# Key stacks of 48 stored rows, with their rows of ones written on chip, in a two-layer attention and expert kernel

## What is computed

```python
x = L0_attn_x
xn = _layernorm(x, axis=-1)
s = attention with 16 heads of 8 channels on xn
g = _silu(mixture of experts on xn)
x = x + s * g
```

## Time and profile before

| | us |
|---|---|
| median of 3 runs | 1200.33 (1199.22 to 1203.84) |
| the profiled execution | 1205.69 |
| its span in the trace | 1203.9 |
| PE busy | 1068.8 |
| DVE busy | 814.8 |
| ACT busy | 646.0 |
| POOL busy | 201.9 |

### The profile page before, as it was taken

The page is one execution under the profiler, slowest core; times in us unless marked ns, Lnnn a source line. Parts: engine busy times, 40 slices in busy tenths (PEclk is TensorE's granted clock), DMA queues, the critical chain, the costliest instruction groups (busy, mean ns, idle before and its releaser), DMA issues.

```text
span 1203.9 us, 19384 instructions
## 1 busy us (share of the span) xinstructions
PE 1068.8 (89%) x7308; PEld 496.2 (41%) x7308; DVE 814.8 (68%) x1621; ACT 646.0 (54%) x1258; POOL 201.9 (17%) x323
## 2 busy tenths in 40 slices
PE   5799999999999999999864799889989999988767
PEld 4455555552222222222233343334444478444444
DVE  6656666667887888883377587888872255565654
ACT  4522222217898888989622256667775533432534
POOL 2244554510010101011000001123320000000000
PEclk9799999999999999999976688999997999998888
DMA  4674121000110110000034013211322020000431
GB/s 117 206 227 140 49 79 66 1 10 19 30 42 29 43 32 27 18 13 21 10 122 142 28 39 80 76 48 50 129 97 80 11 79 1 1 1 0 142 141 35
DMA packets 57398, 74.63 MB, mean 62 GB/s; under 512 B 15720, under 2 KB 35032, under 8 KB 55512
## 3 DMA queue, kind: packets, MB, share of 16 engines
q1 hardware_dynamic: 48516, 62.13, 16.2%
q10 hardware_dynamic: 8788, 11.26, 3.2%
HBM read 58.18 MB, written 14.54 MB: 60 GB/s over the span
## 4 chain that ended last, share of the span: by engine, by line
PE 70%; DVE 18%; ACT 7%; issue 3%; DMA 1%; ACTq 0%; SPq 0%; POOL 0%; DVEq 0%
PE PS L1806 68%; DVE mx L1575 9%; ACT arena L1074 5%; PE PS L1819 1%; DVE arena L1374 1%; DVE arena L1780 1%; PE PS L2278 0%; DVE arena L1377 0%; DVE arena L1338 0%; DVE arena L1326 0%; DVE small L1766 0%; DMA arena<-mrow 0%; DMA arena<-in_L_attn_x 0%; ACT arena L1027 0%; DVE fw L1671 0%
## 5 line engine op out<-in xcount | busy, mean ns | idle before, releaser
L1806 PE MATMUL PS<-arena 128*32 128x512 f32 (+12 forms) x3656 | 565.8, 474 | 60.9 <-DVE mx L1575 23.4
L1575 DVE TENSOR_REDUCE mx<-PS 128x1 f32<-128x512 f32 (+3 forms) x896 | 512.3, 623 | 82.8 <-PE PS L1806 78.6
L1074 ACT ACTIVATE arena<-PS 128x512 f32<-128x512 f32 (+3 forms) x896 | 435.4, 559 | 149.7 <-PE PS L1806 145.7
L1806 PEld LDWEIGHTS PS<-arena 128*32 128x32 f32 (+3 forms) x3656 | 147.1, 104 | 416.9 <-ACT arena L1074 183.8
L1806 PE MATMUL PS<-x_hi,w_hi_lo 128*128 128x512 f32 x320 | 145.5, 496 | 7.0 <-POOL x_lo L991 2.6
L1117 ACT ACTIVATE fw<-PS 128x512 f32<-128x512 f32 x80 | 47.8, 597 | 168.1 <-PE PS L1806 168.1
L1671 DVE TENSOR_TENSOR fw<-PS,fw 128x512 f32<-128x512 f32 x80 | 55.3, 692 | 79.1 <-PE PS L1806 75.1
L1806 PE MATMUL PS<-fw 128*128 128x512 f32 (+3 forms) x184 | 99.2, 625 | 0.0
L985 POOL TENSOR_TENSOR fw<-fw,arena 128x512 f32<-128x512 f32 x64 | 81.8, 1280 | 75.7 <-DVE fw L1671 75.7
L917 POOL TENSOR_TENSOR arena<-arena,fw 128x512 f32<-128x512 f32 x31 | 39.8, 1284 | 296.6 <-DMA fw<-sum_dram 296.6
L1806 PEld LDWEIGHTS PS<-x_hi,w_hi_lo 128*128 128x128 f32 x320 | 61.2, 191 | 38.4 <-issue 21.5
(11 more groups left out here) (315 smaller groups left out, 1113.9 us busy)
## 6 DMA issues: line engine op xcount, KB each, us to landing
arena<-comb_dram SPq DMA_DIRECT2D x14, 1024.0 KB, 4.9
arena<-comb_dram SPq DMA_DIRECT2D x18, 512.0 KB, 7.3
fw<-sum_dram SPq DMA_DIRECT2D x31, 256.0 KB
q_dram<-arena SPq DMA_DIRECT2D x24, 256.0 KB, 4.0
k_dram<-arena SPq DMA_DIRECT2D x24, 256.0 KB, 4.2
arena<-k_dram ACTq DMA_DIRECT2D x20, 204.0 KB
arena<-q_dram ACTq DMA_DIRECT2D x20, 192.0 KB
arena<-drev_dram SPq DMA_DIRECT2D x16, 192.0 KB, 6.8
```

The lines of the kernel that those rows point to most:

```text
L1074: s.activation(Pr[:, m % 8, 0:w], st_bank(l, m, 0, w), ACT.Exp).then_inc(A["e_done"], 1)
L1575: v.reduce_max(mx[:, H % 2, kh, n:n + 1], bank(ring_bank[l][U], 0, w), axis=AX.X, negate=True).then_inc(A["ring_free"], 1)
L1806: return nc.tensor.matmul(out_, lhsT, rhs, start=start, stop=stop)
```

## The change

The key stacks are stored with 48 rows, so that the DMAs of store_qk write with another stride and those of load_group read 48 rows (192 KB) instead of 51. The two DMAs that stored the rows of ones are gone. In their place POOL sets whole regions of the arena to one before any key stack is loaded into them: 16 KiB of each of the 128 partitions (8192 bf16 elements) from 48 KiB on, at the start, after the memsets of Vst; and the same amount from 32 KiB on in layer 1's attention, after the maxima of H = 0 and 1 and before the loop over the halves. A load overwrites 48 rows at partition 0 and 48 at partition 64; the three rows after each keep their ones. SP and ACT wait for the first memset where they waited for the stores of ones, and ACT waits for the second before it loads group 4 of layer 1. The old ones region (96 x 1024 bf16) and POOL's wait behind it are gone. The matmuls are the same.

```diff
-        k_dram = [dram(f"k_dram{l}", (GROUPS * HG, TROWS, SEQ), BF16) for l in range(2)]
+        k_dram = [dram(f"k_dram{l}", (GROUPS * HG, ROWS, SEQ), BF16) for l in range(2)]
...
-        ones_rows = bf(62, 2)[0:32 * PARTS, :]
+        ones_rows = [bf(48, 16), bf(32, 16)]
...
-                dr, rows, at_ = ((q_dram[l], ROWS, q_at[l]), (k_dram[l], TROWS, k_at[l]))[piece % 2]
-                src = bass.AP(tensor=dr.tensor, offset=(G * HG + hh) * rows * SEQ,
-                              ap=[[SEQ, rows], [2 * rows * SEQ, PAIRS], [1, SEQ]])
-                dst = bf(at_[G], 4)[64 * hh:64 * hh + rows, :].rearrange("p (r t) -> p r t", r=PAIRS)
+                dr, at_ = ((q_dram[l], q_at[l]), (k_dram[l], k_at[l]))[piece % 2]
+                src = bass.AP(tensor=dr.tensor, offset=(G * HG + hh) * ROWS * SEQ,
+                              ap=[[SEQ, ROWS], [2 * ROWS * SEQ, PAIRS], [1, SEQ]])
+                dst = bf(at_[G], 4)[64 * hh:64 * hh + ROWS, :].rearrange("p (r t) -> p r t", r=PAIRS)
...
-            sp.wait_ge(zero_done, 3)
-            for l in range(2):
-                dst = bass.AP(tensor=k_dram[l].tensor, offset=ROWS * SEQ, ap=[[TROWS * SEQ, GROUPS * HG], [SEQ, PARTS], [1, SEQ]])
-                sp.dma_start(dst, ones_rows).then_inc(ones_stored, 16)
             store_qk(sp, 0, 0)
...
-            sp.wait_ge(ones_stored, 16 * 2)
+            sp.wait_ge(ones_set, 1)
...
                 for H in range(LAG[l]):
                     max_parts(H)
+                pool.wait_ge(z_ready, 12)
+                g.memset(ones_rows[1], 1.0).then_inc(ones_set, 1)
                 for H in range(HALVES):
...
             pool.wait_ge(const_done, 1)
-            g.memset(ones_rows, 1.0).then_inc(zero_done, 1)
-            pool.wait_ge(zero_done, 3)
             own.link(g.memset(Vst[:, :, :, :, :], 0.0))
             own.link(g.memset(Vst[:, :, :, :, HD:HD + 1], 1.0))
...
+            g.memset(ones_rows[0], 1.0).then_inc(ones_set, 1)
             weights_lo(0)
...
-            act.wait_ge(ones_stored, 16 * 2)
+            act.wait_ge(ones_set, 1)
...
                 act.wait_ge(last_norm, 1)
+                act.wait_ge(ones_set, 2)
                 next_group(1, 4, (0, 1))
```

More of the change, by code:

```diff
@@ L472, in block_net @@
             "lg_ps", "gx_ready", "ge_ready", "comb_ready", "cb_ps", "cb_ev"))
-        comb_stored, ones_stored = sem("comb_stored"), sem("ones_stored")
+        comb_stored, ones_set = sem("comb_stored"), sem("ones_set")
         rows_ps, rows_ev = sem("rows_ps"), sem("rows_ev")
@@ L614, in store_qk @@
                 for n in range(parts):
-                    dst = bass.AP(tensor=k_dram[l].tensor, offset=(b * HEADS * TROWS + (row + n) * HD) * SEQ,
-                                  ap=[[TROWS * SEQ, HEADS], [SEQ, HD], [1, SEQ]])
+                    dst = bass.AP(tensor=k_dram[l].tensor, offset=(b * HEADS * ROWS + (row + n) * HD) * SEQ,
+                                  ap=[[ROWS * SEQ, HEADS], [SEQ, HD], [1, SEQ]])
                     src = kspb[b][:, n, :] if l else ksp[:, n, b * SEQ:(b + 1) * SEQ]
```

## The result

| | before | after |
|---|---|---|
| median of 6 runs each, us | 1201.16 (1199.06 to 1203.84) | 1208.49 (1207.02 to 1210.19) |
| the profiled execution, us | 1205.69 | 1207.02 |
| its span, us | 1203.9 | 1205.2 |

The ratio is 1.006, with a 95% interval of 1.0041 to 1.008: the change costs 7.2 us. Lines of the kernel after are 2 to 4 lower (L1332 is the L1334 of before, L1804 its L1806, L1071 its L1074, L679 and L597 are unchanged).

A forecast was written before the change was run, and what follows sets the result against it. PE (70% of the chain of waits) and DVE (18%) were taken to bound the kernel; +5.2 - 3.0 + 2.2 = +4.4 us on 1200.33 gave 1204.7 us, with 8 in 10 for 1197.0 to 1211.0.

The forecast's parts named there:

- Spared stores: At the start, dropping the two stores of ones from SP's queue gains nothing, since the serial start covers them.
- First memset: At the start, POOL's 6.97 us memset holds DVE's tensor_scalar L1334 until 15.93 instead of 10.72, delaying the serial start: +5.2 us.
- rival of a clock that falls at the later start: After longer PE idling at the start, a low clock doubles 3.4 us of projection matmuls: +7.8 at most, chance 0.10.
- Two-input instructions held as well: Rival: beside the first memset DVE's two-input instructions also wait, +5.8 in place of +5.2, 1205.3 us, chance 0.05.
- Short hold: Rival: DVE gets in between parts of the long first memset, so the sum is -1.8, 1198.5 us; chance 0.15.
- Maxima rows: At layer 1's attention start, 48-row key loads finish before the maxima rows load, so PE goes on earlier: -3.0 us.
- rival of late rows: At layer 1's attention start, group loads still collide with the maxima rows; the 3.0 is not gained: +7.4, chance 0.15.
- Second memset: In layer 1's attention, POOL's 6.97 us memset exceeds 4.70 us idle, delaying PE's matmul of the H = 2 maxima: +2.2 us.
- Key loads elsewhere are covered: Key loads away from layer 1's start change nothing, as PE is the chain while layer 0's groups 1 to 3 load.
- other waits between 54 and 600 us: Sign of a wrong forecast: new waits in PE's list in this stretch, where the same time as before was expected.
- a fifth of 0.55: Share of the forecast (0.50) and two-input (0.05) cases counted as slower by over 0.5%, put at 0.12.

The follow-up runs named there:

- e1: Kernel after, first memset written as float32 words holding two bf16 ones, half by DVE early and half by POOL: ratio 1.0023 to before.
- e4: Kernel before plus one POOL memset of 8192 bf16 elements in an unused region, behind the memsets of Vst: ratio 1.0049, +5.9 us.
- e8: Kernel before with 48-row key stacks only in layer 1, its memset between the maxima of H = 0 and 1: ratio 0.9980, -2.4 us.
- e2: Kernel after with POOL's second memset moved between the maxima of H = 0 and 1: ratio 1.0044 to before.
- e12: Kernel before plus only the second memset (8192 bf16 elements, behind the maxima of H = 0 and 1): ratio 1.0017, +2.0 us.
- e7: Kernel after with 48-row key stacks only in layer 0, first memset split between DVE and POOL, no second memset: ratio 1.0025 to before, +3.0 us.
- e10: Kernel after with layer 0's loads of groups 4 to 7 issued by SP instead of ACT, both long memsets kept: ratio 1.0032 to before.
- e3: Kernel after with first memset split between DVE and POOL and second memset between the maxima of H = 0 and 1: ratio 1.0004 to before.
- e5: e3 with layer 0's loads of groups 4 to 7 issued by SP instead of ACT: ratio 0.9989 to before, -1.3 us.
- e11: e5 with the second memset written as 4096 float32 words holding two bf16 ones: ratio 0.9979 to before, -2.5 us.

## Why the prediction was right in part, and what it missed

The direction and the range held, and so did the terms of the first memset and of the maxima rows; the second memset was right in its mechanism and uncertain in its size. The size of the whole did not hold: 4.4 us were forecast and 7.2 came, which is just over 0.5%, where I had thought a change within 0.5% likelier. Step by step:

- **Spared stores: nothing.** No run takes this by itself, and none tells against it; SP's new waits appear nowhere in the chain.
- **First memset, +5.2 us: right.** Its length 6.92 us (forecast 6.97), its place 8.94 (8.93), L1332's end 15.89 (15.93). Of the 5.17 us, 3.8 are left when PE takes over; the ratios give 4.4 (after against e1). The rival of a clock that falls at the later start did not come: transposes and projections ran at 1.00, as before. It had priced the eight projections at 3.4 us; they took 4.24 before and 3.45 after.
- **Two-input instructions held as well: false.** They took 0.17 and 0.19 us in the memset. The Trainium skill's rule on this ("GPSIMD Engine Reference", section Key points) counts both kinds; beside a memset the measurement decides against it for two-input instructions. The Trainium skill also says ("VectorE: DVE Perf Modes", section Mode 2×_2P — use both read ports for one tensor) that a float32 tensor_scalar from SBUF uses both read ports, which tensor_tensor can't. The trace agrees with the half that concerns the tensor_scalar: 6.35 us for one that takes 0.17.
- **Short hold: false**, from the same line, and e4 shows it with nothing else changed.
- **Maxima rows, -3.0: right**, -2.73 in the chain's piece (4.50 to 1.77), -2.4 by e8's ratio. The piece is 4.01 to 4.53 us in the five traces with 51 rows in layer 1 and 1.77 to 1.80 in the nine with 48. The rival of late rows had asked for under 150 GB/s; the loads moved at 154 to 217 in the full windows and were nearly over when the last of the maxima loads was issued at 681.90.
- **Second memset, +2.2: the mechanism right, the size at most that.** PE waits for POOL behind the memset, and the two matmuls are 8.20 to 8.21 us apart in all four kernels with the memset at this place. Against the kernel before that is +1.94. But 6.26 us is the shortest such distance of all ten kernels without it; the others have 6.81 to 7.66, and e2, which only moves the memset, has 7.33. So the memset's own price was 0.5 to 1.9 us, 0.9 by e2's trace. The ratios (+2.0 by e12, +1.9 by e2) are within their intervals of all of this. The prediction let the memset fill 4.70 us of idle time that it had from a single trace.
- **"Key loads elsewhere are covered: PE is the chain while groups 1 to 3 of layer 0 come in": the step that failed.** It looked at the transfers of three groups and at nothing that issues them. Groups 4 to 7 of layer 0 are issued by ACT between exponentials that PE waits for, and for these I had put nothing. In the trace after, six of these eight key issues take 0.44 or 0.45 us and two 0.98 and 1.26, where seven took 0.33 and one 0.54; the two long ones stand in the chain. Price: +3.0 by e7, +3.4 by e10, and +1.3 to +3.2 us between the marks in the five traces that have these issues. The prediction had named the sign, other waits between 54 and 600 us, where it expected the same time as before. In the kernel before nothing shows that an issue can take 1.0 us, but the row of ACT's 0.33 us for group 2 was there, and a bound from it (eight key issues of layer 0, each doubled: 8 x 0.33 = 2.6 us) would have put the sum at 7.0; the doubling is chosen with hindsight.

By the ratios the sum now reads 4.4 + 2.0 + 3.2 - 2.4 = 7.2 us: first memset, second memset, layer 0's issues (mean of e7 and e10), maxima rows. It meets the measured 7.2. The terms come from different sittings and each has an uncertainty of 2 to 3 us, and the traces have less for the second memset, so the close meeting is luck in part; what carries the account is that every term has its line in a trace and that each taken away alone moved the time the way it should. One slip in the chances changes nothing: a fifth of 0.55 is 0.11, not 0.12.

Open: why some back-to-back issues take 0.44 us and others 0.98 to 1.57. In e7 three of the first five take 0.88 or more, in e3 two, with the same loads. Part of the cost in layer 0 is the clock that falls behind a long stop (0.50 at 406 to 408 us after and at 400 to 402 in e7, 0.56 at 400 to 402 in e1, 1.00 all along in e2 and e3). Layer 0's attention costs 2.9 to 3.2 us more in the three traces where it falls and 1.3 and 1.8 in the two where it doesn't; what decides whether it falls is open.

## What to carry to other kernels

A transfer that is hidden still has an issue, and that one lies on the engine that issues it: when a DMA's shape changes, read the duration of its issue and ask what is queued behind it, or spread the issues, or give them to an engine that nobody waits for. A long memset on POOL is not free in POOL's idle time: choose a time at which DVE runs no tensor_scalar from SBUF, and write float32 words that hold two bf16 values, which halves it. Price a fill by its slot in the list as well: the same memset made PE wait at one place and was hidden one item earlier. And compare traces stretch by stretch between fixed marks: that showed 0.4 us in layer 0's attention, where the ratio of whole executions could not tell 2 us from nothing.

## What the runs showed of the hardware that I had not expected

- In layer 0's attention a DMA of 48 rows issued by ACT right behind another of 48 rows took 0.43 us or more to issue, up to 1.57 us; with four exponentials between the two it took 0.31, and right behind a key load of 51 rows the next query load took 0.37 and 0.38 us in layer 1 before. On SP most pairs took 0.48 and 0.43 us, but single key issues took 1.18 (e10), 1.58 (e5), 1.52 and 1.37 us (e11); so the long ones are not ACT's alone.
- POOL's memset goes by elements, not bytes: 8192 bf16 in 6.92 us, 4096 float32 words, the same bytes, in 3.51, 2048 in 1.80.
- One DVE instruction took 6.35 us, until 0.03 us behind the end of a memset, while the two ahead of it, which have two inputs, ran inside the same memset in 0.19 and 0.17 us.
